# Rows normalised and split to 16 bits in the attention, and turned by transposing DMAs instead of TensorE, in a gated attention and mixture-of-experts kernel

## The reference

```python
x = x + jnp.tanh(g_xattn[0]) * xattn(ctx_1024, _layernorm(x), ...)     # q, k, v, softmax, Wout
x = x + jnp.tanh(g_ffn[0]) * ffn(_layernorm(x), gate_w, w1, b1, w2, b2)
# ffn: gate_scores = softmax(xf @ gate_w); the two best, normalised
#      h = gelu(xf @ w1[e] + b1[e]); y = h @ w2[e] + b2[e]; out = sum of the two, weighted
```

## Time and profile before

| | |
|---|---|
| median of 3 runs | 1811.77 us (1811.46 to 1815.03) |
| the profiled execution's own time | 1811.51 us |
| its span | 1809.8 us |
| TensorE, VectorE, ScalarE, GpSimd busy | 92%, 73%, 66%, 69% of the span |
| attention | to about 1357 us |
| chain between attention and tiles | to about 1408 us |
| tiles | to the end |

### The profile page before, as it was taken

One profiled execution on the slowest core, in us unless ns is written; L12 is line 12 of the kernel. 1 busy time (PEld: TensorE's weight loads), 2 busy tenths in 40 slices (PEclk: granted clock), 3 DMA queues, 4 the chain that ended last, 5 costly groups with the idle time before them and its releaser, 6 DMA issues. The chain is left out here.

```text
span 1809.8 us, 42402 instructions
## 1 busy us (share of the span) xinstructions
PE 1663.9 (92%) x15046; PEld 1165.8 (64%) x15046; DVE 1315.1 (73%) x3073; ACT 1199.5 (66%) x2733; POOL 1255.7 (69%) x1349
## 2 busy tenths in 40 slices
PE   1899999999999999999999999999952899999997
PEld 0456666666666666666666666665641779999996
DVE  4677788787878777787777787877745786666664
ACT  2587877877777877777787778776753554444443
POOL 5388777777778888887888878876774244554443
PEclk9999999999999999999999999999975899999999
DMA  4167776777658777766676667755777432232231
GB/s 142 33 140 138 147 148 138 150 147 144 142 126 152 143 139 152 148 134 129 144 147 135 145 129 148 133 105 100 150 148 228 130 78 44 49 48 48 48 48 14
DMA packets 597272, 217.62 MB, mean 120 GB/s; under 512 B 536914, under 2 KB 587904, under 8 KB 596684
## 3 DMA queue, kind: packets, MB, share of 16 engines
q1 hardware_dynamic: 581532, 198.24, 52.5%
q0 software_dynamic: 15536, 16.67, 5.7%
HBM read 67.72 MB, written 16.83 MB: 47 GB/s over the span
## 5 line engine op out<-in xcount | busy, mean ns | idle before, releaser
L524 POOL TENSOR_TENSOR p_parts<-p_space,p_parts 112x487 f16<-112x487 f32 x512 | 559.7, 1116 | 138.3 <-ACT p_parts L662 137.6
L653 ACT ACTIVATE p_space<-scores_ps,shift 112x487 f32<-112x487 f32 x508 | 335.6, 665 | 9.5 <-POOL p_parts L524 6.2
L708 ACT ACTIVATE k_hi<-proj_ps 128x488 fp32r<-128x488 f32 x256 | 148.1, 579 | 270.6 <-PE proj_ps L1122 270.5
L878 DVE TENSOR_SCALAR_CACHE_REDUCE passed<-scores_ps 112x487 f16<-112x487 f32 x502 | 302.3, 659 | 24.5 <-PE scores_ps L1146 24.3
L953 DVE SCALAR_TENSOR_TENSOR v_sb<-proj_ps,v_sb 128x512 f16<-128x512 f32 (+1 forms) x256 | 176.8, 691 | 139.4 <-ACT v_sb L722 138.5
L662 ACT ACTIVATE p_parts<-p_space 112x487 f16<-112x487 f32 x512 | 276.4, 608 | 0.0
L758 ACT ACTIVATE o_space<-scores_ps,b_sb,undo 128x256 f32<-128x256 f32 x280 | 139.7, 560 | 193.4 <-PE scores_ps L1276 186.5
L628 POOL DMA_INDIRECT out_dram<-pt_space,ot_space x70 | 113.6, 1623 | 189.2 <-ACT pt_space L768 165.4
L947 DVE TENSOR_TENSOR k_lo<-proj_ps,k_hi 128x488 fp32r<-128x488 f32 x256 | 169.4, 662 | 92.9 <-ACT k_hi L708 92.5
L1177 PE MATMUL pv_ps<-v_sb,pt_space 128*128 128x128 f16 x2048 | 218.4, 221 | 8.1 <-DVE o_space L999 6.2
L1122 PE MATMUL proj_ps<-kv_hi,wkv_hi 128*128 128x488 f16 x512 | 191.8, 375 | 36.0 <-POOL kv_lo L551 13.5
(11 more groups left out here) (231 smaller groups left out, 3567.3 us busy)
## 6 DMA issues: line engine op xcount, KB each, us to landing
w_part<-in_L_ffn_w_dram SPq DMA_DIRECT2D x64, 256.0 KB
arena<-in_L_ffn_w_dram SPq DMA_DIRECT2D x28, 512.0 KB, 5.1
ctx_sb<-in_ctx_dram SPq DMA_DIRECT2D x32, 375.0 KB
pt_space<-p_parts SPq DMA_TRANSPOSE x256, 4.0
x_sb<-in_x_dram SPq DMA_DIRECT2D x32, 112.0 KB
res_sb<-in_x_dram SPq DMA_DIRECT2D x32, 112.0 KB
out_dram<-x_sb SPq DMA_DIRECT2D x32, 112.0 KB, 2.8
xn_dram<-xn_sb SPq DMA_DIRECT2D x32, 112.0 KB, 2.0
```

The costliest lines, as they stand in the source:

```text
L524: pool.tensor_tensor(p_parts[0:LQ, p % PS, h, 1, 0:LK], p_f[0:LQ, p % 2, h, 0:LK], p_parts[0:LQ, p % PS, h, 0, 0:LK], ALU.subtract).then_i ...
L653: act.activation(p_f[0:LQ, p % 2, h, 0:LK], score_bank(p, h)[0:LQ, 0:LK], ACT.Exp, bias=shift[0:LQ, p // 2 % 2, n:n + 1], scale=-1.0, accu ...
L708: act.activation(k_hi[:, j], ps[:, 0:LKP], ACT.Copy).then_inc(kq_high, 1)
L878: dve.tensor_scalar(passed_of(p, h), score_bank(p, h)[0:LQ, 0:LK], P_SHIFT, None, ALU.add, ALU.min, accum_out=shift[0:LQ, p // 2 % 2, n:n ...
```

## The change

ScalarE copies xn, scaled by 1024, as 16-bit high parts into a new tile xn16 (after the copy of the transposed rows, stage `xnt_copy`), and VectorE writes the low parts next to them (after `top`). Before it writes, ScalarE waits until the store of the batch before has landed. SP stores the two parts together (again 1024 bytes a row) in stage `share` instead of `xnt`. In the tiles, SP turns each gathered half (128 rows of 512 16-bit values) with one transposing DMA straight into the operand's layout, when the rows are there and h of the tile two before is done. TensorE's transposes and VectorE's two steps for each tile are gone. h(n) and the next gather wait for x_turned. SP's loads of units 18 to 27 and 31 move from the plain list into the same loop, behind the turnings. VectorE waits for all stores once before the tiles, since xn16 lies where the experts' parts are written.

```diff
-LAST_LOADS = tuple(range(FIRST_LAST, 18)) + (28, 29, 30) + tuple(range(18, 28)) + (31,)
+LAST_LOADS = tuple(range(FIRST_LAST, 18)) + (28, 29, 30)
...
-            at_("rest4", [128, 384])
+            xn16 = at_("xn16", [128, 768], F16)
...
+        xs_parts = carve(pt_space, 0, [2, 2, 2 * D], F16)
...
-        xt_hi = carve(o_parts_space, 0, [2, KD, ROWS], F16)
-        xt_lo = carve(o_parts_space, 2048, [2, KD, ROWS], F16)
+        xt_sb = carve(o_parts_space, 0, [2, 2 * KD, ROWS], F16)
...
@@ SP
-                    sp.wait_ge(xn_done, ob + 1)
-                    sp.dma_start(xn_rows[ob * LQ:(ob + 1) * LQ], xn_sb[0:LQ, s]).then_inc(stored[s], 16)
+                for ob in batches_at("share", t):
+                    sp.wait_ge(xn_low, ob + 1)
+                    sp.dma_start(xn_rows[ob * LQ:(ob + 1) * LQ], xn_parts(ob).bitcast(F32)).then_inc(stored[ob % 2], 16)
...
+            for t in range(-2, TILES):
+                n = t + 2
+                if n < TILES:
+                    sp.wait_ge(x_read[n % 2], (n // 2 + 1) * 32)
+                    if n >= 2:
+                        sp.wait_ge(h_done, 4 * (n - 2) + 4)
+                    for a in range(2):
+                        sp.dma_start_transpose(xt_sb[:, n % 2, :, a * 128:a * 128 + 128], xs_parts[:, n % 2, a]).then_inc(x_turned[n % 2], 16)
+                for u in TILE_SPLITS.get(t, ()):
+                    if u + 4 < 28:
+                        load_unit(u + 4)
+                    if u == 28:
+                        load_unit(31)
...
@@ GpSimd
-                    pool.wait_ge(xt_done, t + 1)
+                    pool.wait_ge(x_turned[t % 2], (t // 2 + 1) * 32)
...
@@ ScalarE, stage xnt_copy
+                    if ob >= 1:
+                        act.wait_ge(stored[(ob - 1) % 2], 32 * ((ob - 1) // 2 + 1))
+                    act.activation(xn_parts(ob)[:, 0:D], xn_sb[0:LQ, ob % 2], ACT.Copy, scale=X_SCALE).then_inc(xn_high, 1)
...
@@ VectorE, stage top
+                    dve.wait_ge(xn_high, ob + 1)
+                    dve.scalar_tensor_tensor(out=xn_parts(ob)[:, D:2 * D], in0=xn_sb[0:LQ, ob % 2], scalar=X_SCALE, in1=xn_parts(ob)[:, 0:D],
+                                             op0=ALU.mult, op1=ALU.subtract).then_inc(xn_low, 1)
...
@@ VectorE, before and in the tiles
+            for s in range(2):
+                dve.wait_ge(stored[s], NB // 2 * 32)
...
-                if t + 2 < TILES:
-                    s = t % 2
-                    dve.wait_ge(xt_done, t + 3)
-                    rows = xt_ps[:, :].rearrange("p (k t) -> p k t", k=KD)
-                    if t >= 0:
-                        dve.wait_ge(h_done, 4 * t + 4)
-                    dve.tensor_scalar(xt_hi[:, s], rows, X_SCALE, None, ALU.mult).then_inc(xt_high, 1)
-                    dve.wait_ge(xt_high, t + 3)
-                    dve.scalar_tensor_tensor(out=xt_lo[:, s], in0=rows, scalar=X_SCALE, in1=xt_hi[:, s], op0=ALU.mult, op1=ALU.subtract).then_inc(xt_copied, 1)
...
@@ TensorE
-                    pe.wait_ge(xt_copied, n + 1)
+                    pe.wait_ge(x_turned[n % 2], (n // 2 + 1) * 32)
...
-                                                            (xt_hi, xt_lo)[x_][:, n % 2, k], start=(k == i == 0), stop=(k == KD - 1 and i == 2))
+                                                            xt_sb[:, n % 2, KD * x_ + k], start=(k == i == 0), stop=(k == KD - 1 and i == 2))
...
-                if t + 2 < TILES:
-                    n = t + 2
-                    pe.wait_ge(x_read[n % 2], (n // 2 + 1) * 32)
-                    if n >= 1:
-                        pe.wait_ge(xt_copied, n)
-                    for k in range(KD):
-                        for a in range(2):
-                            last = nc.tensor.transpose(xt_ps[:, k * ROWS + a * 128:k * ROWS + a * 128 + 128], xs_sb[:, n % 2, a, k * 128:k * 128 + 128], ident[:, :])
-                    last.then_inc(xt_done, 1)
```

More of the change, by code:

```diff
@@ L278, in program, with xn_parts @@
         tail_bank = bank("tail_ps")
-        h_ps, y_ps, xt_ps = scores_ps, proj_ps, pv_ps
+        h_ps, y_ps = scores_ps, proj_ps
+        def xn_parts(b):
+            return xn16[0:LQ, 0:2 * D]
         def tail_ps(b):
@@ L308, in program @@
         x_read = [sem("x_read0"), sem("x_read1")]
-        xt_done = sem("xt_done"); xt_high = sem("xt_high"); xt_copied = sem("xt_copied"); h_done = sem("h_done"); gelu_done = sem("gelu_done")
+        xn_high = sem("xn_high"); xn_low = sem("xn_low"); x_turned = [sem("x_turned0"), sem("x_turned1")]; h_done = sem("h_done"); gelu_done = sem("gelu_done")
         g_high = sem("g_high"); g_ready = sem("g_ready"); y_done = sem("y_done"); y_ready = sem("y_ready"); y_weighed = sem("y_weighed")
```

## The result

The changed kernel takes 1819.6 us (median of 12 runs, 1810.2 to 1823.2), the kernel before 1811.5 in the same comparison: ratio 1.0033, 95% interval 1.0023 to 1.0043. It is 0.33% slower, where 1799.0 was forecast. The profiled execution took 1821.45, its span 1819.7 (before: 1809.8).

A forecast was written before the change was run, and what follows sets the result against it. TensorE was taken to bound attention and, working in order, the tiles. Terms -14.9 - 2.25 - 1.8 + 0.6 + 0.7 + 1.5 + 0 + 3.6 = -12.55 against 1811.51 gave 1799.0 us, range 1794.5 to 1806.5.

The forecast's parts named there:

- (f): Attention: ScalarE's copy and VectorE's step in each of 32 batches fit in gaps: 0, at worst +29 us.
- C: Rival: the two new attention steps spill over, each batch losing up to 0.90 us, 1828 in full; chance 0.07.
- (e): Early tiles: turnings behind unit loads on SP's queue land late, chiefly at tiles 3 and 4: +1.5 us, 0 to +7.
- (g): End of attention: batch 30's copy waits for batch 29's store, +2.8; batch 31's two new steps, 0.8: +3.6 us.
- (c): Entering the tiles: transposing DMAs replace TensorE's transposes and VectorE's steps; uncovered for tile 0 only: +0.6 us (-1.1 to +2.5).
- Rival D: Slow turnings: two transposing DMAs take 12 us a tile, +41 us in the tiles, 1838; chance 0.04.
- (d): The clock entering the tiles: +0.7 us in the sum.
- (a): Tiles: the transposes after h(0) to h(33) leave TensorE's order, 34 x 0.44: -14.9 us.
- (b): Tiles: the wait before h(1) goes, -2.25 us; before tile 7, gather wait and transposes leave TensorE's order, -1.8 us.

The follow-up runs named there:

- e3: Changed kernel with SP issuing each group of unit loads one iteration later, behind that tile's turning: 1811.4 us, ratio 0.9997.
- e9: e1 with each two units' loads also issued one tile later, behind that tile's turning; real low parts left out: 1796.8 us, ratio 0.9926.
- e2: Changed kernel with VectorE's low step moved before the max, both SBUF inputs kept: 1812.8 us, ratio 1.0007.
- e1: Changed kernel with VectorE's low step reading a PSUM tile (times 0) instead of xn_sb, before the max; real low parts left out: 1800.3 us, ratio 0.9940.
- e7: Changed kernel with the low part made by GpSimd as a subtraction in SBUF, from rows already scaled by 1024: 1805.1 us, ratio 0.9962.
- e11: The changed kernel once more, one run without any edit: 1815.1 us.
- e6: Changed kernel with GpSimd issuing one table scatter a turn instead of two from step 208 on: 1810.6 us, ratio 0.9994.

## Why the prediction was wrong

- **(f), the step that failed.** "Both are inside a gap in that batch: 0, at worst all of 0.90 x 32 = +29." The durations were right (0.42 and 0.40), and 28 of the 32 steps did cost nothing. The other four cost 17.8 us: the step stood beside GpSimd's run of SBUF steps, a wait that the prediction doesn't have. I priced the step by what it takes alone and looked at VectorE's and ScalarE's neighbours in a middle batch, not at GpSimd, whose run behind two scatters stands in the trace of the kernel before. The range left out even (f)'s own bound of +29. C had the right direction and named the right wait, but its mechanism (up to 0.90 us in every batch) was another: 5 us, in few batches, none in most.
- **(e)** was mis-sized: +1.5, range 0 to +7. In the chain, h(2) waits 1.80, h(4) 3.2 (1470.65 to 1473.86) and h(6) 0.74, and h(4) runs at half clock (granted 0.50 from 1474.3 to 1477.7) for part of its 7.08 (+1.84): 7.6 in all. That turnings stand behind loads was the right cause: in e3 and e9, with the loads behind the turnings, the three gaps are gone. By e9 a reordering gets 2.5 to 3.5 of it back. I had looked for it at h(3) and h(4).
- **(g)** was right in place and in what the wait shows at first. ScalarE's timeline, batch 30:

```profile
1380.89 0.42 ACT L725 ACTIVATE xn<-xn_sb 112x256 f16<-112x256 f32 x1 [5.24 <-DMA xn_dram<-xn]
1381.21 0.40 ACT L753 ACTIVATE o_parts_space<-o_space 112x256 f16<-112x256 f32 x1
```

  The o_parts copy comes 22.70 us later than in the earlier trace rows, the tail of batch 30 20.0: +2.7 for a forecast of +2.8. At batch 31's tail only 1.85 are left. From there to the start of the table's read it takes 19.28 us against 17.38, 1.9 more; how much of that is the two new steps' (forecast 0.8) was not tried. Together +3.8 for a forecast of +3.6. It hides behind two transfers that were quicker in this profile, the table's read (6.56 us for 8.26) and the first gather (3.40 for 3.97): -2.3, which is no part of the change that anything here shows.
- **(c)** From the gather's landing to h(0) it takes 4.24 us (1426.14 to 1430.38) against 2.99 before: +1.25, forecast +0.6. The first turning is 1.2 on SP, and the second lands 2.7 after its issue begins. Rival D, with 12 us a tile, is out: tile 0's two turnings (eight 128x128 blocks) took 4.0 us from the first issue to the last landing.
- **(d)**, the clock entering the tiles, had the wrong sign. The +0.7 that the sum takes for it was an estimate that no run shows; in its place the runs showed -1.2: h(0) and h(1) take 12.08 us for 10.48, 1.6 too long (granted clock 0.52 from 1430.38 to 1433.50, 1.00 from there), where h(0) alone was 2.8 too long before (0.50 from 1404 to 1412). The half clock came back later, in h(4), behind the 3.2 us wait (it is counted in (e)).
- **(a) and (b)** came as said: 10.48 us a tile, h(1) directly behind h(0), and the wait for the last unit's split stays before h(7).

The tiles' terms together: -14.9 - 2.25 - 1.8 - 1.2 + 7.6 = -12.6, measured -12.8. With (c), (g) and the quicker transfers that is -12.6 + 1.25 + 3.8 - 2.3 = -9.85, and the 17.8 of (f) on top make +8.0. The spans differ by 9.9, 2.2 of it from the start of the profile: +7.7; the medians by 8.1. The point at which attention decides was said to be 0.39 us a batch, 12.5 in all; it was passed by four instructions.

## What to carry to other kernels

A VectorE step with two SBUF inputs beside a busy GpSimd can cost up to the rest of GpSimd's unbroken run of SBUF steps, not just its own duration: here up to 5.46 us (5.81 in e2) for 0.41, beside a run of 5.94. Look for such runs in the trace before; give the step a PSUM input (at most 0.42 us in e1), or put it on GpSimd itself (0.66, once 1.64, in e7), and look at the maximum beside the median of its line. A mean or a middle batch doesn't show it: the cost sits in the few batches in which the schedule shifts. When work is taken from TensorE and put behind a queue, read that queue's whole order around it, and then the order of the queue that is late next.

## What the runs showed of the hardware

- A blocked step can be shut out at the ends of several GpSimd instructions. In batch 23 it came 0.36 us before the end of the first of six, went in at none of their ends, and ended 0.28 us after the last. But in 26 batches of e2 it came some 0.40 us before such an end and was let in there (0.67 us), and in batch 28 of the changed kernel it was let in before the last step of the run (L550), after 5.23 us. So the moment of its coming alone does not decide. In batches 0 to 26 of the seven profiles with two SBUF inputs, what GpSimd did in front of that pair of steps parts the two kinds without exception: it had stood idle 0.38 to 3.61 us where the low step was let in at the first end (176 steps), and at most 0.03 us, straight from a scatter, where it was shut out (13 steps). Why that matters was not tried.
- The long time is booked as VectorE's busy time (5.46 us in batch 23), with no wait beside it. The waits that follow name the engine that was blocked (TensorE waits 14.9 us in all for VectorE's q_lo), not the one that blocks; GpSimd's five large steps in that run take their usual 1.10 to 1.13 us.
- A wait of TensorE of a few us can be paid twice, by a half clock behind it. Behind the 3.2 us before h(4) its 48 matmuls took 7.08 us, with the granted clock at 0.50 from 1474.3 to 1477.7, and behind e9's 4.45 before h(7) 6.79 (0.57 from 1482.65 to 1486.00). Behind waits of 2.02 to 3.40 us it went either way: 7.08 in e7 (2.05 before h(3) and 2.23 before h(7)), 5.41 at full clock in e11 (3.40 before h(4)), 5.41 or 5.42 in e1, e3, e6 and both kernels. Behind no wait or one of at most 1.80, h(0) aside, it was 5.24 to 5.50. What makes the clock fall was not tried.
